# Softmax attention of a two-layer model: heads in two 64-row tiles, masks of the maxima on VectorE, PV in pairs of units

## The reference

```
qkv = x @ w_attn;  q, k, v = split(qkv)          # 16 heads of 16
attn = einsum('bhqd,bhkd->bhqk', q, k) / sqrt(16)
attn = where(causal, attn, -inf)                  # 1024 x 1024 a head
out = einsum('bhqk,bhkd->bhqd', softmax(attn), v) @ w_proj
```

## Time and profile before

| | us |
|---|---|
| median of 3 runs (4137.22 to 4146.11) | 4139.46 |
| profiled execution, span from first to last instruction | 4136.6 |
| busy: TensorE / VectorE / ScalarE / GpSimd | 3388.8 / 2384.2 / 1507.4 / 839.8 |
| softmax attention, start of the first and of the last score matmul (L578) | 303.9 and 1411.0 |

### The profile page before, as it was taken

The page is one execution under the profiler, slowest core; times in us unless marked ns, Lnnn a source line. Parts: engine busy times, 40 slices in busy tenths (PEclk is TensorE's granted clock), DMA queues, the critical chain, the costliest instruction groups (busy, mean ns, idle before and its releaser), DMA issues. The chain is left out here.

```text
span 4136.6 us, 62031 instructions
## 1 busy us (share of the span) xinstructions
PE 3388.8 (82%) x21377; PEld 2546.4 (62%) x21377; DVE 2384.2 (58%) x5007; ACT 1507.4 (36%) x2286; POOL 839.8 (20%) x1006
## 2 busy tenths in 40 slices
PE   6859999999999766579564776999566599999998
PEld 5735555555555465569343564777466488888887
DVE  5546666666666377683123785555477644444544
ACT  2315555555555433334002662000133323333333
POOL 0021111111111122234674663000122100000000
PEclk9879999999999878789656998999777699999999
DMA  6884666666666256563565996666344433233331
GB/s 191 234 146 60 85 85 85 85 81 84 84 85 84 74 184 200 183 214 127 132 139 138 345 346 217 210 207 206 108 153 153 158 84 85 86 81 81 81 81 51
DMA packets 452026, 570.37 MB, mean 138 GB/s; under 512 B 94544, under 2 KB 300400, under 8 KB 450672
## 3 DMA queue, kind: packets, MB, share of 16 engines
q1 hardware_dynamic: 440064, 544.45, 52.3%
q0 software_dynamic: 10240, 14.16, 2.0%
q10 hardware_dynamic: 1648, 10.81, 0.7%
HBM read 329.62 MB, written 238.61 MB: 137 GB/s over the span
## 5 line engine op out<-in xcount | busy, mean ns | idle before, releaser
L493 DVE TENSOR_REDUCE att_mx<-att_m_ps 128x1 f32<-128x512 f32 (+4 forms) x1248 | 743.5, 645 | 381.6 <-PE att_m_ps L554 324.1
L523 ACT ACTIVATE att_pr<-att_e_ps 128x1024 f32<-128x1024 f32 (+3 forms) x768 | 597.7, 811 | 366.5 <-PE att_e_ps L578 362.3
L551 PE MATMUL att_m_ps<-att_ks,att_qs 128*128 128x512 f32 (+3 forms) x1536 | 470.3, 377 | 99.5 <-PEq L39 95.4
L578 PE MATMUL att_e_ps<-att_qs,att_ks 128*128 128x512 f32 (+3 forms) x1536 | 466.9, 386 | 10.5 <-PEq L39 9.0
L475 POOL TENSOR_SCALAR_AFFINE_SELECT att_pr<-att_pr 128x256 f32<-128x256 f32 x512 | 206.7, 407 | 938.5 <-PEq L571 931.9
L578 PEld LDWEIGHTS att_e_ps<-att_qs,att_ks 128*128 128x128 f32 x1536 | 249.1, 194 | 239.9 <-issue 186.7
L551 PEld LDWEIGHTS att_m_ps<-att_ks,att_qs 128*128 128x128 f32 x1536 | 280.0, 195 | 155.2 <-issue 93.7
L594 PE MATMUL att_o_ps<-att_pr,att_vs 128*17 128x512 f32 (+3 forms) x3072 | 330.1, 502 | 0.0
L2116 DVE TENSOR_TENSOR ffn_hid<-ffn_gate,ffn_u_ps 128x512 f32<-128x512 f32 x192 | 132.1, 688 | 249.5 <-PE ffn_u_ps L698 213.1
L2164 ACT ACTIVATE ffn_hh<-ffn_hid 128x512 fp32r<-128x512 f32 x192 | 121.4, 633 | 421.5 <-DVE ffn_hid L2120 319.3
L698 PE MATMUL ffn_y_ps<-ffn_wld,ffn_hh 128*128 128x256 f32 x768 | 216.9, 282 | 0.0
(11 more groups left out here) (286 smaller groups left out, 8168.2 us busy)
## 6 DMA issues: line engine op xcount, KB each, us to landing
prj_o<-attended SPq DMA_DIRECT2D x32, 1024.0 KB, 5.0
ffn_wt<-weights SPq DMA_DIRECT2D x16, 2048.0 KB, 16.0
att_qs<-q_high SPq DMA_DIRECT2D x64, 256.0 KB, 5.8
att_qs<-q_low SPq DMA_DIRECT2D x64, 256.0 KB, 8.7
att_ks<-k_high SPq DMA_DIRECT2D x64, 256.0 KB, 12.3
att_ks<-k_low SPq DMA_DIRECT2D x64, 256.0 KB, 15.9
attended<-att_ot SPq DMA_DIRECT2D x64, 256.0 KB, 2.2
prj_x<-x SPq DMA_DIRECT2D x32, 512.0 KB, 5.9
```

The costliest lines, as they stand in the source:

```text
L493: e.reduce_max(mx[:, h, heads[0]:heads[-1] + 1, q], src, AX.X).then_inc(m_free, 1)
L523: e.activation(pr[:, u % NPR, 2 * p:2 * p + 2, 0:w], e_ps[:, s % 2, :, 0:w], ACT.Exp).then_inc(exp_done, 1)
L551: ins = e.matmul(out[:, i], qs[:, j, hd, q * P:(q + 1) * P], ks[:, j, hd, h * BLK:h * BLK + w], start=i == 0, stop=h != q // 4, skip_group ...
L578: i = e.matmul(e_ps[:, s % 2, n, 0:w], ks[:, j, hd, k * P:(k + 1) * P], qs[:, j, hd, (h + 1) * BLK - w:(h + 1) * BLK], start=True, stop=True)
```

## The change

The stacks hold two heads: head n (0 or 1) of a pair on partitions 64n to 64n + 63. Three products of the parts stand there instead of four, (qh, qh, ql) against (kh, kl, kh), 48 rows. Rows 48 to 62 are zeros against ones, row 63 (`MAXROW`) the maxima against ones. `qs` and `ks` are 128 x NBUF x 2 x T. Scores use 64 rows, maxima 63, and the two heads of a pair are two matmuls on different rows of the array, into different banks. Every maxima piece is one head wide: 24 pairs, 48 pieces. The diagonal pieces are not masked by a matmul: VectorE adds a causal tile of 512 columns and takes the maximum in one instruction (`tensor_tensor_reduce`), 32 of the 48 pieces; the other 16 stay a reduce. Units up to 256 wide are one step of all four heads, so there are 20 steps. PV runs in front of every even unit for the two units 4 and 3 back, with 32 value columns a head (the next head's columns, or zeros, fill up). NBUF is 4, `pr` has 6 buffers, LAG is 3, the row of maxima is two DMAs, and a load is 13 DMAs. New memsets set the ones and zeros at the start, and all loads but the first follow them.

```diff
-    NBUF = 3
-    NPR = 4
+    NBUF = 4
+    NPR = 6
     MBUF = 3
-    SR = 4 * HD
+    LAG = 3
+    HALF, MAXROW, VSTEP = P // 2, P // 2 - 1, GH * VW + 32 - VW
...
+        qs = ph.sb("qs", [P, NBUF, 2, T], f32r)
+        ks = ph.sb("ks", [P, NBUF, 2, T], f32r)
+        vs = ph.sb("vs", [P, NBUF, KB, VSTEP])
+        pr = ph.sb("pr", [P, NPR, 2, 2, BLK])
...
+        units = [(h, k) for h in range(2) for k in range(4 * h + 4)]
+        UNITS = len(units)
+        steps = []
+        for u, (h, k) in enumerate(units):
+            steps += [(u, (0, 1))] if width(h, k) <= BLK // 2 else [(u, (0,)), (u, (1,))]
...
+        whole, partial = [], []
         for q in range(KB):
             for h in range(q // 4 + 1):
-                per = max(1, min(GH, BLK // (min(BLK, (q + 1) * P - h * BLK))))
-                if (q, h) == (1, 0):
-                    pieces += [(q, h, (0, 1)), (q, h, (2,)), (q, h, (3,))]
-                else:
-                    pieces += [(q, h, tuple(range(n, n + per))) for n in range(0, GH, per)]
-        NPC, MEND, MAXIMA = len(pieces), 19, 20
-        assert NPC % MBUF == 0
-        def width(h, k):
-            return BLK - max(0, k * P - h * BLK)
-        def keys(q, h):
-            return min(BLK, (q + 1) * P - h * BLK)
-        def diagonal(s):
-            h, k, p = steps[s]
-            return k * P >= h * BLK
+                (partial if h == q // 4 else whole).extend((q, h, p) for p in range(2))
+        pairs, taken = [], 0
+        for n, piece in enumerate(partial):
+            pairs.append(piece)
+            while taken < len(whole) and taken + 1 <= len(whole) * (n + 1) / len(partial):
+                pairs.append(whole[taken])
+                taken += 1
+        NPAIR, NPC = len(pairs), 2 * len(pairs)
+        TURN, MAXIMA = 8, 16
...
-                    for name, dst, parts in (("qh", qs, (0, 1)), ("ql", qs, (2, 3)),
-                                             ("kh", ks, (0, 2)), ("kl", ks, (1, 3))):
-                        for r in parts:
-                            e.dma_start(dst[r * HD:(r + 1) * HD, j].bitcast(fp32), src_rows[name][g]
-                                        ).then_inc(stack_loaded[j], 16)
-                    e.dma_start(vs[:, j], v_rows[g]).then_inc(stack_loaded[j], 16)
-                    e.dma_start(maxima_row(j), zero[:]).then_inc(stack_loaded[j], 16)
+                    for n in range(2):
+                        for dst, parts in ((qs, ("qh", "qh", "ql")), (ks, ("kh", "kl", "kh"))):
+                            for r, name in enumerate(parts):
+                                at = n * HALF + r * HD
+                                e.dma_start(dst[at:at + HD, j].bitcast(fp32), src_rows[name][g][:, 2 * n:2 * n + 2]
+                                            ).then_inc(stack_loaded[j], 16)
+                    e.dma_start(vs[:, j, :, 0:GH * VW], v_rows[g]).then_inc(stack_loaded[j], 16)
                 def row(j):
                     e.wait_ge(nmt_ready, 1)
-                    e.dma_start(maxima_row(j), nmt[:].bitcast(fp32)).then_inc(mrow_loaded, 16)
+                    for n in range(2):
+                        at = n * HALF + MAXROW
+                        e.dma_start(qs[at:at + 1, j].bitcast(fp32).rearrange("o h (k p) -> o (h k) p", p=P),
+                                    nmt[16 * n:16 * n + 16].bitcast(fp32)).then_inc(mrow_loaded, 16)
...
+                e.memset(ks[32:HALF, 0].bitcast(fp32), 1.0).then_inc(first_ones, 1)
+                e.memset(qs[32:HALF, 0].bitcast(fp32), 0.0).then_inc(first_ones, 1)
+                e.memset(ks[32:HALF, 1:].bitcast(fp32), 1.0).then_inc(later_ones, 1)
+                e.memset(qs[32:HALF, 1:].bitcast(fp32), 0.0).then_inc(later_ones, 1)
+                e.memset(vs[:, :, :, GH * VW:].rearrange("p j k c -> p (j k) c"), 0.0).then_inc(consts_pe, 1)
...
-                    for n, (q, h, heads) in enumerate(pieces):
-                        w = keys(q, h)
+                    for n in range(NPC):
+                        q, h, p = pairs[n // 2]
+                        w, at = keys(q, h), 2 * (n % 2) + p
                         e.wait_ge(m_scores, n + 1)
-                        src = m_ps[:, n % MBUF, 0:len(heads) * w].rearrange("p (n w) -> p n w", w=w)
-                        e.reduce_max(mx[:, h, heads[0]:heads[-1] + 1, q], src, AX.X).then_inc(m_free, 1)
+                        if h == q // 4:
+                            e.tensor_tensor_reduce(kept[:, n % MBUF, 0:w], m_ps[:, n % MBUF, 0:w], causal[:, BLK - w:], 1.0,
+                                                   -3e38, ALU.add, ALU.max, mx[:, h, at, q:q + 1]).then_inc(m_free, 1)
+                        else:
+                            e.reduce_max(mx[:, h, at, q:q + 1], m_ps[:, n % MBUF, 0:w], AX.X).then_inc(m_free, 1)
...
-                def piece(j, n):
-                    q, h, heads = pieces[n]
+                def maxima_pair(j, i):
+                    q, h, p = pairs[i]
                     w = keys(q, h)
-                    e.wait_ge(m_free, n + 1)
-                    out = m_ps[:, n % MBUF, 0:len(heads) * w].rearrange("p (n w) -> p n w", w=w)
-                    for i, hd in enumerate(heads):
-                        ins = e.matmul(out[:, i], qs[:, j, hd, q * P:(q + 1) * P], ks[:, j, hd, h * BLK:h * BLK + w],
-                                       start=i == 0, stop=h != q // 4, skip_group_check=True)
-                    if h == q // 4:
-                        ins = e.matmul(out[:, :, w - P:w], identb[:],
-                                       causal[:].unsqueeze(1).broadcast_to((P, len(heads), P)), start=False,
-                                       stop=True, skip_group_check=True)
-                    ins.then_inc(m_scores, 1)
-                    if n == NPC - 1:
+                    for n in range(2):
+                        e.wait_ge(m_free, 2 * i + n + 1)
+                        rows = slice(n * HALF, n * HALF + MAXROW)
+                        e.matmul(m_ps[:, (2 * i + n) % MBUF, 0:w], qs[rows, j, p, q * P:(q + 1) * P],
+                                 ks[rows, j, p, h * BLK:h * BLK + w], start=True, stop=True).then_inc(m_scores, 1)
+                    if i == NPAIR - 1:
                         take(e, (m_free, NPC))
...
-                    for n in range(2):
-                        hd = 2 * p + n
-                        i = e.matmul(e_ps[:, s % 2, n, 0:w], ks[:, j, hd, k * P:(k + 1) * P],
-                                     qs[:, j, hd, (h + 1) * BLK - w:(h + 1) * BLK], start=True, stop=True)
+                    for m, p in enumerate(ps):
+                        for n in range(2):
+                            rows = slice(n * HALF, n * HALF + MAXROW + 1)
+                            i = e.matmul(e_ps[:, s % 2, n, m * w:(m + 1) * w], ks[rows, j, p, k * P:(k + 1) * P],
+                                         qs[rows, j, p, (h + 1) * BLK - w:(h + 1) * BLK], start=m == 0,
+                                         stop=m == len(ps) - 1, skip_group_check=True)
                     i.then_inc(e_scores, 1)
...
-                        i = e.matmul(o_ps[32 * hd:32 * hd + VW, BLK - w:BLK], vs[:, j, k, hd * VW:(hd + 1) * VW],
-                                     pr[:, u % NPR, hd, 0:w], start=k == 0, stop=k == 4 * h + 3)
+                        i = e.matmul(o_ps[32 * hd:32 * hd + 32, BLK - w:BLK], vs[:, j, k, hd * VW:hd * VW + 32],
+                                     pr[:, u % NPR, hd // 2, hd % 2, 0:w], start=k == 0, stop=k == 4 * h + 3)
...
+                    for u in range(UNITS):
+                        if u % 2 == 0 and not (first and u < LAG + 1):
+                            products(j, u - LAG - 1)
+                            products(j, u - LAG)
+                        if u == TURN and more2:
                             e.wait_ge(stack_loaded[nxt2], LOADS)
                             take(e, (stack_loaded[nxt2], LOADS))
-                        if more2 if s >= MEND else more:
-                            for n in share[s]:
-                                piece(nxt2 if s >= MEND else nxt, n)
-                        if s % 2 and not (first and s < 2 * LAG):
-                            products(j, s // 2 - LAG)
-                    take(e, (exp_done, len(steps)), (masked, NDIAG))
+                        due = list(share[u]) if (more2 if u >= TURN else more) else []
+                        for s in of_unit[u]:
+                            for i in due[:1]:
+                                maxima_pair(nxt2 if u >= TURN else nxt, i)
+                            due = due[1:]
+                            exponentials(s, first)
+                            if s == MAXIMA and more:
+                                maxima()
+                            scores(j, s)
+                        for i in due:
+                            maxima_pair(nxt2 if u >= TURN else nxt, i)
+                    take(e, (exp_done, NS), (masked, NDIAG))
```

(23 more changed lines are left out.)

137 lines of the change are left out of this document (65 added, 72 removed).

## The result

The changed kernel takes 4199.6 us (median of 4 runs, 4179.2 to 4203.9) against 4141.4 for the kernel before on the same chip: ratio 1.0134, 95% interval 1.0108 to 1.0159. The forecast was 3992. The profiled execution has a span of 4195.2 us, 58.6 more than before. By the starts of the transposes (L563 before, L580 after) the 58.6 us divide so: from the start to the first in the steady run -5.0, thirty periods of 36.8 us instead of 35.1 +50.9, from the last transpose to the last product +12.3, everything behind the attention +0.4. All of it lies in the stage that was changed.

A forecast was written before the change was run, and what follows sets the result against it. TensorE's own instructions were taken to bound the kernel at 35.0 us a group; afterwards VectorE's 26.5 + 3.6 + 0.1 = 30.2 us would. Over 31 groups that saves 148 us: 4139.5 - 148 = 3992 us, range 3905 to 4095.

The forecast's parts named there:

- What bounds the kernel now: Steady groups of 35.0 us: bound by TensorE's own instructions, 31.6 us plus 0.3 for the transpose, the other 3.1 waits.
- Row-tile pairs: Scores and maxima on TensorE: two heads side by side bring 96 matmuls from 17.9 us a group to 9.0 to 10.6.
- rival B: Score and maxima pairs do not run side by side; 33 us a group, 4077 us; chance 0.12.
- Masks: Masks of the maxima moved to VectorE: TensorE loses 2.1 us of work a group.
- PV in pairs: Six PV blocks a group instead of twelve on TensorE, saving 6 x 0.33 = 2.0 us a group.
- Rival C: TensorE's clock falls, 0.4 of the time at 1.2 GHz: 3 us more a group, 4084 us; chance 0.09.
- VectorE's work 25.6: Per group on VectorE: 23.0 us for 48 maxima pieces plus 2.6 for the add-and-maximum's extra cost.
- drain, gaps and row: Per group on VectorE: 0.85 us drain and combine, 3.6 gaps around PV blocks, 0.1 for the row of maxima.
- second result: Maximum given by VectorE's causal-tile add: 0.08 us for each of 32 pieces, 2.6 us a group; bounds 0 and 0.19 each.
- rival D: VectorE's add-and-maximum runs at half rate: 39.8 us a group, 4288 us, slower than before; chance 0.07.
- Start and loads: Kernel start and operand loads: cost 0, once, with loads hidden; bounds 12.9 us more and 5 less.
- The range: Whole kernel: 3905 to 4085 us from fixed cost (-80 to +109) and gaps (-65 to +74), widened to 4095.

The follow-up runs named there:

- single_four_buffers: The pe_unrolled kernel with the PV of one unit in front of every unit instead of two before every second; 4005.5 us, ratio 0.969 to the kernel before.
- pe_unrolled: The changed kernel with TensorE's loop written out, 28 groups in a line, all else as it is; 4159.5 us, ratio 1.005 to the kernel before.

## Why the prediction was wrong, by its steps

- **"What bounds the kernel now": incomplete.** "The other 3.1 of 35.0 are waits" was left unread. 2.0 of them (52.7 us in 26 groups) are the wait for the loads. The change has a fourth buffer, so this did not hurt the sum, but it made TensorE's own instructions look like the only bound.
- **Row-tile pairs (17.9 to 9.0-10.6): right in kind, size not reached.** Pairs can run side by side, so rival B falls, but in the changed kernel fewer than half start together. TensorE's own work did not fall to the 19 to 20.5 us of the sum, 21 to 22.5 with twelve blocks: it is busy 27.2 us a group in single_four_buffers (762.12 us in 28 groups from 388.5 us). Pipeline tails explain only part of that: in the kernel before the same way of counting gives 31.9 where 33.1 are busy. TensorE never was as free as the sum had it.
- **Masks (2.1 on TensorE): 1.3 where it could be measured.** In the sum it did not count.
- **PV in pairs (-2.0 us a group): the step that failed.** TensorE was forecast not to be the bound, so the 2.0 were worth nothing, and what the long blocks do to the clock was put at nothing. The cost was +5.1 us a group (35.8 against 30.7) at a clock of 0.79 for 0.98, 154 us between pe_unrolled and single_four_buffers. Undoing the pairs in the changed kernel gives 134.
- **Rival C, the clock: right in kind and in share, far off in price.** It put 0.4 of the time at 1.2 GHz; the thirty groups have a mean clock of 0.80, which is 2 x (1 - 0.80) = 0.40 of the time. But it charged only four PV blocks, 3 us, and set the chance at 0.09 on the ground that "the last group, with long waits for ScalarE, keeps 1.00". That row is of a kernel with full-array matmuls and a PV block every unit. The same group keeps 0.94 to 1.00 with single units (27.1 and 25.9 us) and falls to 0.67 with pairs, 35.8 us; that was costed at nothing too.
- **A term that was missing: the loop's instructions.** +1.0 us a group here (36.8 against 35.8), 40 us; 60 in the faster kernel. The page on the kernel before shows the queue with 42 packets, and its loop of three groups fetches none; the change made it four groups, and I counted DMAs and buffers of that step but not instructions. The Trainium skill, Advanced Engine Details and Errata, section "ISA Cache", gives TensorE 128 KB in lines of 16 KB. A turn of this loop fetches 9 packets of 16 KB, 147 KB, and stalls; but the same code in a straight line takes 38 packets in 856 us, an estimated 104 KB for four groups, which would fit. So the page points at the place to look and does not by itself tell that four groups are too many.
- **VectorE's work 25.6 and its idle time 4.6: two errors that cancel.** The second result costs nothing (0.610 us start to start at 512 columns; its 83 ns read runs beside the next operation), so the 2.6 us are not there and rival D falls: 0.69 us busy, not 1.2. In single_four_buffers VectorE is busy 24.0 us a group (670.88 us in 28 groups) and idle 6.7, where drain, gaps and row were put at 0.85 + 3.6 + 0.1. Sum 30.7 for 30.2; that it is so near is luck.
- **Start and loads (0): right.** The first score is 3.7 us earlier.
- **The range.** Its two bounds, 80 and 65 us down and 109 and 74 up, give 3889 to 4124 if added as squares, not 3905 to 4085. The result is outside both.

Before the two edits are separated the forecast thus misses by 208 us: the pairs 154 (the last group's 9 in it), the fetch 40, VectorE's terms and the rest 13. The order of the edits moves some 20 us from one to the other, as the 134 and 154 show. That the 154 are the clock's doing is not shown in full: with doubled maxima on both sides 15 of them are left, 10 of these in the last group.

## What to carry over

When a change takes work off the engine that was the bound, ask what its clock does once it waits, and price the whole stretch at the lower level, not a few blocks; here it paid to keep its long bursts spread out. Count the instructions in a loop's body when it grows. And read the wait behind the bound before trusting a gain: an edit on TensorE worth 7 us with three buffers was worth 38 with four.

## What the runs showed of the hardware

- The same TensorE work a group, 144 matmuls of the program, takes 30.5 us in nearly every group at 0.98 with twelve short PV blocks and 34 to 40 us at 0.79 with six long ones. Redundant matmuls can pay: 48 more a group make the kernel 40 us faster with the long blocks, and 99 slower with the short ones.
- A stall for instructions is 5.6 to 7.0 us once per turn of a loop that fetches 147 KB a turn; the same code in a straight line fetches 38 packets in 856 us and shows no such stall. A loop of three groups fetches none.
- A tensor_tensor_reduce of 512 fp32 columns, one source in PSUM, takes VectorE the time of a plain reduce, 0.61 us from start to start.
- At the start of the kernels on the old stacks the DMA of a 16 KB row into one partition, issued behind the queued loads, holds SyncE's queue for 11.9 to 12.9 us. A third load with its row ahead of the first maxima moved the first score back by 19 us.
